# Second batch's reciprocals in step eight, gate rows ahead of the next rows' scaling, reciprocals' loads sent before the rows

## The reference, cut to what matters

```python
x = layernorm(x + attention(x, wq, wk, wv, wo))
# the feed-forward part, xf = x as 4096 rows
h = xf @ gw1.T + gb1
h = relu((h - mean(h)) * rsqrt(var(h) + 1e-5) * gamma + beta)      # 32 wide
gates = h @ gw2.T + gb2                                            # 8 wide
top_v, top_i = top_k(gates, 2); top_g = softmax(top_v)
onehot = (top_i[..., None] == arange(8)); counts = onehot.sum(axis=0)
w = einsum('nke,nk,ke->ne', onehot, top_g, counts <= capacity)
tmp = einsum('ni,eir->enr', xf, lora_A) * w.T[:, :, None]
out = xf @ weight.T + einsum('enr,ero->no', tmp, lora_B) / 16
x = layernorm(x + out)
```

## Time and profile before

| what | us |
|---|---|
| median of 3 runs | 3506.47 (3506.14 to 3508.07) |
| the profiled execution | 3506.97 |
| its span on the core | 3505.2 |
| mean granted clock of TensorE | 0.99 |

### The profile page before, as it was taken

The page is one execution under the profiler, slowest core; times in us unless marked ns, Lnnn a source line. Parts: engine busy times, 40 slices in busy tenths (PEclk is TensorE's granted clock), DMA queues, the critical chain, the costliest instruction groups (busy, mean ns, idle before and its releaser), DMA issues.

```text
span 3505.2 us, 61763 instructions
## 1 busy us (share of the span) xinstructions
PE 3426.8 (98%) x25202; PEld 2411.1 (69%) x25202; DVE 2013.6 (57%) x3618; ACT 1459.9 (42%) x1830; POOL 1743.8 (50%) x747
## 2 busy tenths in 40 slices
PE   8999998999999999999999999999998999999999
PEld 7888885566666666666665666666657888878887
DVE  3122116777777667677777767767655666642222
ACT  3111111555555555555555555555542332221111
POOL 0000002888988988898898898889550000000000
PEclk9999997999999999999999999999999999999999
DMA  6334325111121111112112111110037777654553
GB/s 214 114 123 120 113 90 127 26 51 48 32 54 50 35 42 50 42 34 51 48 32 54 50 31 47 50 38 11 26 106 217 234 234 234 211 201 173 173 173 130
DMA packets 248172, 340.60 MB, mean 97 GB/s; under 512 B 55520, under 2 KB 150240, under 8 KB 247904
## 3 DMA queue, kind: packets, MB, share of 16 engines
q1 hardware_dynamic: 247904, 336.87, 32.2%
HBM read 203.08 MB, written 133.17 MB: 96 GB/s over the span
## 4 chain that ended last, share of the span: by engine, by line
PE 78%; DVE 2%; ACT 2%; DMA 1%; issue 1%; POOL 0%; SPq 0%; ACTq 0%; POOLq 0%; DVEq 0%
PE p_o L682 19%; PE p_qm L647 17%; PE p_km L675 12%; PE p_acc L42 7%; PE p_acc L44 7%; PE p_acc L43 7%; PE p_km L668 3%; PE p_qm L651 2%; PE p_km L670 2%; ACT p_probs L759 2%; DVE p_part_max L795 1%; PE p_ag_ps L1096 1%; PE p_acc L1085 1%; DMA p_recip<-reciprocals 1%; PE p_ag_ps L1097 1%
## 5 line engine op out<-in xcount | busy, mean ns | idle before, releaser
L795 DVE TENSOR_REDUCE p_part_max<-p_qm 128x1 f32<-128x512 f32 (+3 forms) x2240 | 1407.0, 670 | 579.5 <-PE p_qm L647 328.8
L618 POOL TENSOR_TENSOR p_psums<-p_psums,p_probs 128x1024 f32<-128x1024 f32 x620 | 1479.3, 2386 | 93.3 <-ACT p_probs L755 2.8
L759 ACT ACTIVATE p_probs<-p_km 128x1024 f32<-128x1024 f32 x896 | 878.5, 1021 | 481.0 <-PE p_km L675 430.8
L647 PE MATMUL p_qm<-p_k_st,p_q_st 96*128 96x512 f32 (+3 forms) x2560 | 913.8, 421 | 12.4 <-DMA p_q_st<-q_hi 10.8
L647 PEld LDWEIGHTS p_qm<-p_k_st,p_q_st 96*128 96x128 f32 x2560 | 481.8, 195 | 254.2 <-issue 112.9
L675 PE MATMUL p_km<-p_q_st,p_k_st 97*128 97x512 f32 x1792 | 599.9, 417 | 13.5 <-ACT p_probs L759 8.7
L682 PE MATMUL p_o<-p_probs,p_v 128*32 128x256 f32 (+1 forms) x9216 | 565.5, 372 | 0.0
L682 PEld LDWEIGHTS p_o<-p_probs,p_v 128*32 128x32 f32 x9216 | 271.5, 110 | 216.7 <-issue 45.2
L675 PEld LDWEIGHTS p_km<-p_q_st,p_k_st 97*128 97x128 f32 x1792 | 312.1, 192 | 112.6 <-ACT p_probs L759 74.7
L614 POOL TENSOR_TENSOR p_psums<-p_probs 128x1024 f32<-128x1024 f32 x110 | 262.1, 2383 | 223.9 <-ACT p_probs L759 223.9
L33 POOL MEMSET p_ident<- 128x128 f32 x2 | 0.4, 204 | 551.0 <-POOLq L64 543.2
(11 more groups left out here) (153 smaller groups left out, 4004.0 us busy)
## 6 DMA issues: line engine op xcount, KB each, us to landing
p_q_st<-q_hi SPq DMA_DIRECT2D x128, 256.0 KB, 4.6
p_x_raw<-in_xT SPq DMA_DIRECT2D x64, 256.0 KB, 3.4
q_hi<-p_out_hi SPq DMA_DIRECT2D x64, 256.0 KB, 2.0
q_lo<-p_out_lo SPq DMA_DIRECT2D x64, 256.0 KB, 2.3
p_q_st<-q_lo SPq DMA_DIRECT2D x64, 256.0 KB, 4.3
attended_T<-p_o_raw SPq DMA_DIRECT2D x128, 128.0 KB
p_a_raw<-attended_T SPq DMA_DIRECT2D x32, 512.0 KB, 4.3
p_recip<-reciprocals SPq DMA_DIRECT2D x128, 128.0 KB, 6.6
```

The source lines that it names most:

```text
L618: pool.tensor_tensor(sums[:, :, :], sums[:, :, :], probs[(n * NS + s) % PB][:, :, :], ALU.add).then_inc(added, 1)
L647: last = pe.matmul(bank[:, x * keys:(x + 1) * keys], q_st[par][0:ROWS, c, h + x, sub * P:(sub + 1) * P], k_st[par][0:ROWS, j * CK:j * CK + ...
L759: act.activation(tile[:, :, :].rearrange("p h q -> p (h q)"), km[s % 2][:, :, :].rearrange("p a b -> p (a b)"), ACT.Exp, scale=SCALE).then ...
L795: dve.reduce_max(part_max[c][:, h:h + heads, sub, j], qm[bank_of(i)][:, 0:item_width(i)].rearrange("p (h k) -> p h k", h=heads), AX.X).the ...
```

## The change

Four things are changed.

1. The denominators of a batch are laid out as 128 x 512 instead of 64 x 1024 (`den0` on its first rows, `den1`), with four loads and four stores instead of two of each, in `Opening` and in `feed_forward`.
2. The second batch's reciprocal is taken out of the opening of VectorE's program. It is done in two halves of 128 x 256 at the ends of steps 6 and 7, stored by SP in step 8, and waited for in step 14, ahead of the loads of block 16.
3. VectorE does `hidden_out` and (from step 4 to the last block) `route` ahead of `divide_a` and `split_a`, with `route` between `hidden` and `hidden_out`; ScalarE does `hidden_root` ahead of `split_a`.
4. SP sends the four loads of reciprocals of block t+2 when block t+1 is scaled, and the load of the rows, behind them, when it is split.

```diff
--- before.py
+++ after.py
@@ -244,7 +244,7 @@
         self.a_raw, self.recip = sb("p3_a_raw", [P, KC, P]), sb("p3_recip", [P, KC, P])
         self.a_hi0 = sb("p3_a_hi0", [P, KC, P], F32R)
         with ExitStack() as until_split:
-            self.den0 = until_split.enter_context(nc.sbuf_tensor("p3_den0", [P, D], F32))
+            self.den0 = until_split.enter_context(nc.sbuf_tensor("p3_den0", [P, S // 4], F32))
         self.a_lo0 = sb("p3_a_lo0", [P, KC, P], F32R)
         with ExitStack() as until_last_chunks:
             tmp = lambda name, shape, dt=F32: until_last_chunks.enter_context(nc.sbuf_tensor(name, shape, dt))
@@ -272,16 +272,16 @@
         sp.dma_start(self.wo_raw[n][:, :], self.wo[n * P:(n + 1) * P, :]).then_inc(self.wo_in[n], 16)
 
     def load_denominators(self, sp):
-        for q in range(2):
-            sp.dma_start(self.den0[q * NH:(q + 1) * NH, :], self.den_d[:, q * D:(q + 1) * D]).then_inc(self.den_in[0], 16)
+        for q in range(4):
+            sp.dma_start(self.den0[q * NH:(q + 1) * NH, :], self.den_d[:, q * BANK:(q + 1) * BANK]).then_inc(self.den_in[0], 16)
 
     def send_reciprocals(self, sp):
         sp.wait_ge(self.rec_done[0], 1)
-        for q in range(2):
-            sp.dma_start(self.rec_d[:, q * D:(q + 1) * D], self.den0[q * NH:(q + 1) * NH, :]
+        for q in range(4):
+            sp.dma_start(self.rec_d[:, q * BANK:(q + 1) * BANK], self.den0[q * NH:(q + 1) * NH, :]
                          ).then_inc(self.rec_stored[0], 16)
         sp.dma_start(self.a_raw[:, :, :], self.aT_d[:, 0:P].rearrange("(k p) t -> p k t", p=P)).then_inc(self.a_in, 16)
-        sp.wait_ge(self.rec_stored[0], 32)
+        sp.wait_ge(self.rec_stored[0], 64)
         for h in range(REP):
             sp.dma_start(self.recip[h * HD:(h + 1) * HD, :, :],
                          self.rec_d[h:NH:REP, 0:P].unsqueeze(0).to_broadcast([HD, KC, P])).then_inc(self.a_in, 16)
@@ -301,8 +301,8 @@
             dve.tensor_tensor(self.wo_lo[:, n, :], self.wo_raw[n][:, :], self.wo_hi[:, n, :].bitcast(F32), ALU.subtract
                               ).then_inc(self.wo_lo_done, 1)
 
-        dve.wait_ge(self.den_in[0], 32)
-        dve.reciprocal(self.den0[0:2 * NH, :], self.den0[0:2 * NH, :]).then_inc(self.rec_done[0], 1)
+        dve.wait_ge(self.den_in[0], 64)
+        dve.reciprocal(self.den0[:, :], self.den0[:, :]).then_inc(self.rec_done[0], 1)
         for n in range(4):
             split_wo(n)
         dve.wait_ge(self.a_in, 16 * (1 + REP))
@@ -893,6 +893,8 @@
         weights = sb("p3_weights", [P, NT, E])
         second = sb("p3_second", [P, NT, E])
         LB = 4
+        with ExitStack() as first_pass:
+            den1 = first_pass.enter_context(nc.sbuf_tensor("p3_den1", [P, S // 4], F32))
         lowB = [sb(f"p3_lowB{i}", [P, ER]) for i in range(LB)]
         lw = [sb(f"p3_lw{i}", [P, ER]) for i in range(2)]
         lwT_hi = [sb(f"p3_lwT_hi{i}", [ER, P], F32R) for i in range(2)]
@@ -901,7 +903,7 @@
         YB, TB = 4, 3
         with ExitStack() as until_wm:
             tmp = lambda name, shape, dt=F32: until_wm.enter_context(nc.sbuf_tensor(name, shape, dt))
-            den1, ag_raw = tmp("p3_den1", [P, D])[:, :], tmp("p3_ag_raw", [P, KC, AG])[:, :, :]
+            ag_raw = tmp("p3_ag_raw", [P, KC, AG])[:, :, :]
         wm_hi, wm_lo = sb("p3_wm_hi", [P, KC, D], F32R), sb("p3_wm_lo", [P, KC, D], F32R)
         yB = [t[:, :] for t in opening.yB]
         lb_raw, lb_hi, lb_lo = opening.lb_raw[:, :], opening.lb_hi[:, :], opening.lb_lo[:, :]
@@ -956,6 +958,8 @@
             return 3 * n + 3
 
         assert wm_step(KC - 1) < NT - 2
+        REC_AT = 7
+        assert REC_AT + 1 < NT // B - 2
 
         def gpsimd(pool):
             over(pool)
@@ -968,6 +972,8 @@
             def load_a(t):
                 sp.dma_start(a_raw[:, :, :], aT_d[:, t * P:(t + 1) * P].rearrange("(k p) t -> p k t", p=P)
                              ).then_inc(a_in, 16)
+
+            def load_recip(t):
                 for h in range(REP):
                     sp.dma_start(recip[h * HD:(h + 1) * HD, :, :],
                                  rec_d[h:NH:REP, t * P:(t + 1) * P].unsqueeze(0).to_broadcast([HD, KC, P])
@@ -991,8 +997,8 @@
             load_x(0)
             load_x(1)
             sp.dma_start(ag_raw, ag.rearrange("(k p) r -> p k r", p=P)).then_inc(ag_in, 16)
-            for q in range(2):
-                sp.dma_start(den1[(2 + q) * NH:(3 + q) * NH, :], den_d[:, (2 + q) * D:(3 + q) * D]).then_inc(den_in, 16)
+            for q in range(4):
+                sp.dma_start(den1[q * NH:(q + 1) * NH, :], den_d[:, S + q * BANK:S + (q + 1) * BANK]).then_inc(den_in, 16)
             sp.dma_start(gw2T[:, :], gw2T_in).then_inc(small_in, 16)
             sp.dma_start(rows[:, :], rows_in.to_broadcast([P, ROWS])).then_inc(small_in, 16)
 
@@ -1010,14 +1016,17 @@
                     sp.wait_ge(y_done, u + 1)
                     sp.dma_start(y_t[u, :, :], y[u % 2][:, :]).then_inc(y_stored[u % 2], 16)
                 if t + 2 < NT:
+                    if t + 2 == NT // B:
+                        sp.wait_ge(rec_stored, 64)
+                    sp.wait_ge(a_done, t + 2)
+                    load_recip(t + 2)
                     sp.wait_ge(a_lo_done, t + 2)
                     load_a(t + 2)
-                if t == 1:
-                    sp.wait_ge(rec_done, 1)
-                    for q in range(2):
-                        sp.dma_start(rec_d[:, (2 + q) * D:(3 + q) * D], den1[(2 + q) * NH:(3 + q) * NH, :]
+                if t == REC_AT + 1:
+                    sp.wait_ge(rec_done, 2)
+                    for q in range(4):
+                        sp.dma_start(rec_d[:, S + q * BANK:S + (q + 1) * BANK], den1[q * NH:(q + 1) * NH, :]
                                      ).then_inc(rec_stored, 16)
-                    sp.wait_ge(rec_stored, 32)
                 for n in range(KC):
                     if t == wm_step(n) - 2:
                         if n > 0:
@@ -1246,10 +1255,10 @@
                     copy_hidden(t - 4)
                 if 1 <= t <= NT:
                     normalize(t - 1)
+                if 3 <= t < NT + 3:
+                    hidden_root(t - 3)
                 if t + 1 < NT:
                     split_a(t + 1)
-                if 3 <= t < NT + 3:
-                    hidden_root(t - 3)
                 for n in range(KC):
                     if t == wm_step(n):
                         split_wm(n)
@@ -1386,14 +1395,20 @@
                     scale_shift((t - 1) % 2, std_done, t, shift_done)
                 if 3 <= t < NT + 3:
                     hidden(t - 3)
+                if 4 <= t < NT:
+                    route(t - 4)
+                if 3 <= t < NT + 3:
+                    hidden_out(t - 3)
+                if NT <= t < NT + 4:
+                    route(t - 4)
                 if t + 1 < NT:
                     divide_a(t + 1)
-                if t + 1 < NT:
                     split_a(t + 1)
-                if 3 <= t < NT + 3:
-                    hidden_out(t - 3)
-                if 4 <= t < NT + 4:
-                    route(t - 4)
+                if t in (REC_AT - 1, REC_AT):
+                    cols = slice(0, BANK // 2) if t < REC_AT else slice(BANK // 2, BANK)
+                    if t < REC_AT:
+                        dve.wait_ge(den_in, 64)
+                    dve.reciprocal(den1[:, cols], den1[:, cols]).then_inc(rec_done, 1)
                 for n in range(KC):
                     if t == wm_step(n):
                         split_wm(n)
@@ -1430,8 +1445,6 @@
             dve.wait_ge(ag_hi_done, 1)
             dve.tensor_tensor(ag_w[:, :, AG:2 * AG], ag_raw, ag_w[:, :, 0:AG].bitcast(F32), ALU.subtract
                               ).then_inc(ag_lo_done, 1)
-            dve.wait_ge(den_in, 32)
-            dve.reciprocal(den1[2 * NH:4 * NH, :], den1[2 * NH:4 * NH, :]).then_inc(rec_done, 1)
             dve.wait_ge(small_in, 32)
             dve.wait_ge(experts_done, 1)
             for t in range(1, NT + 3):
```

## The result

The changed kernel takes 3493.10 us (median of 6 runs, 3490.32 to 3493.86), the kernel before 3506.43 beside it (6 runs, 3505.66 to 3508.07): a ratio of 0.9960, 95% interval 0.9948 to 0.9971, or 13.3 us less. The forecast was 12.4 less, 3494.1. The profiled execution took 3493.86 with a span of 3492.1, against 3505.2 before: 13.1 less.

What follows compares the result with a forecast made beforehand. TensorE, busy 98% of the span, was taken as the bound; removing two stalls of 4.65 and 7.8 us, other terms 0, took 12.4 from 3505.2 to a 3492.8 us span, 3494.1 as median; range 3491.5 to 3500.

Steps and rivals of the forecast that it cites:

- What was at stake: First pass of the feed-forward part: two TensorE stalls near 2632 and 2667 us, together 12.4 us, and nothing else.
- undisturbed step: TensorE's step from turn to turn, 14.46 us; without gate rows and a gate matmul pair, 12.03 us.
- The reciprocal leaves the opening: VectorE's opening: without the 6.55 us reciprocal, y is ready at 2626.8, 3.7 us before TensorE needs it.
- first stall: TensorE before the first turn of y: 2.9 us of wait plus the slow stretch behind it, 4.65 us.
- second stall: TensorE before the first turn of hidden rows: 5.7 us of wait plus 2.07 of slow clock, 7.8 us.
- Loads of blocks 3 and 4: Queue's sooner loads: blocks split by 2644.9 and 2658.1 at the slowest, cover 0.6 and 1.5 us, cost 0.
- The slowest of everything: Worst case for these loads: block 2 split at 2631.7, then 1.1 issue, 8.6 landing, 3.49 scaling and splitting.
- The moved reciprocals: VectorE, steps 6 and 7: two of 128x256, 1.6 us each by columns, 3.3 by elements; covered.
- The gate ahead of the scaling: VectorE's new order waits for TensorE's gate; gate to split 5.9 us, leaving 2.7 us of cover, cost 0.
- third rival: The gate makes scaled rows late in steps 4 to 30, beyond 2.7 us of cover: slower, e.g. 3521; chance 0.06.
- the first: Rival: TensorE waits for block 4's split rows instead of hidden rows; gain 5.3 to 9.3, 3497 to 3501; chance 0.10.

Runs made afterwards that it cites:

- layout only: Kernel before with only the second batch's denominators laid out as 128x512, one reciprocal still in the opening, its stores awaited in step 1: 3503.95 us, ratio 0.9990.
- order only: Kernel before with only the new order: gate rows ahead of scaling on VectorE, the root ahead of the split on ScalarE: 3505.65 us, ratio 0.9992.
- two more: Changed kernel with two idle 128x256 reciprocals on VectorE ahead of the scaling in steps 4 to 30: 3529.07 us, ratio 1.0058 to the kernel before.

## Why the prediction was right

**What was at stake**: right. Two stalls, each a wait and a slow stretch behind it, are all of the gain; 5.04 and 12.97 us at their two marks against 4.65 and 12.4. Most of the first difference is the undisturbed step: 2641.86 - 2630.08 = 11.78 us, where I had 12.03. I set the estimate by the Trainium skill (TensorE: Matmul & The Clock Gate, "HAM oscillation"), 13.7, aside for the 12.4 of the rows; the measured 13.1 of the span lies between them, and the spread of the runs doesn't tell which is nearer.

**The reciprocal leaves the opening**: right, and shown by half of it (layout only): 3.2 us less of VectorE ahead of y is enough for the first stall. In the changed kernel TensorE doesn't wait for y, with the turn at 2630.08.

**What ended the second stall**: here a step failed, though the number stood. "That removes what TensorE waited for at 2670" gave the second stall to VectorE's order. The order alone removes that wait and puts another of 3.8 us in its place; the queue's wait, moved alone, makes the hidden rows 3.9 us earlier with the order unchanged. I had read the 7.0 us of the earlier trace rows and written "that goes", at a cost of 0 and not as the gain. What I should have asked of the earlier trace rows: VectorE stood 5.76 us for block 4's loads, so when were those loads issued, and beside what. They were issued in time and landed late, in the crowd that the queue's wait had held back. The new order is insurance for hidden rows against late loads, and with early loads there is nothing to insure.

**Loads of blocks 3 and 4**: the end was right, a term was not. "The slowest of everything" took 8.6 us for a landing. Issued at 2629.31 and at 2642.69, the raw rows took these, from the transfers by issue of the changed kernel:

```profile
p_a_raw<-attended_T SPq DMA_DIRECT2D x1, 512.0 KB, 9.8
```

```profile
p_a_raw<-attended_T SPq DMA_DIRECT2D x1, 512.0 KB, 11.1
```

The bounds of 2644.9 and 2658.1 still held (2642.67 and 2657.44), because block 2 was split at 2629.28 and not at my 2631.7, so that everything started 2.4 us sooner. The two misses went against each other. Landings now end with the raw rows and no longer with the reciprocals (the bracket of VectorE's rows). The Trainium skill says in DMA: Bandwidth & Descriptors, "Queues, rings and completion order", that a transfer's semaphore write lands only after all earlier writes of its DMA engine, which agrees with this; but the raw rows are also issued last, and whether the rule or the plain load of the engines, at a DMA share of 0.75 to 0.79, sets the time, no run here separates.

**The moved reciprocals**: 1.75 us each, against 1.6 taken and 3.3 as the far bound. Their stores take the queue 5.42 us for four, above my 4.4; TensorE waited for nothing behind it. From the timelines of VectorE and of the queue, changed kernel:

```profile
2700.11 1.75 DVE L1411 RECIPROCAL p_den<-p_den 128x256 f32<-128x256 f32 x1
```

```profile
2729.83 5.42 SPq L1028 DMA_DIRECT2D reciprocals<-p_den  x4
```

**The gate ahead of the scaling**: right. VectorE now waits for TensorE's gate in 30 steps, 2.4 at the longest, and once more for 6.2 at the end of the pass. The third rival's mechanism is real: its break point lies a little nearer than I put it (2.3 to 2.5 against 2.7, as gate to split takes 6.05 us and not 5.9, and TensorE comes 0.1 sooner). The changed kernel stays 1.75 us or more away from it from step 4 on. In step 3, where loads decide, the cover is 1.5 us.

**Rivals**: the first showed itself in order only (a wait for split rows instead of hidden rows) and the third in two more; neither in the changed kernel. Not tried: both new orders together with the reciprocal left in the opening, and the halved reciprocal there together with the moved wait. So what the moving itself adds to these two isn't measured.

## What to carry to other kernels

A wait on the queue that issues transfers holds back all that is queued behind it and then lets it go at once, beside whatever is sent next. When an engine stands for a load, look at when that load was issued, what was issued just ahead of it, and what the queue stood for before that; and move such a wait to where its result is read. Reordering the engine that waits gains only what the load itself leaves, and a later release of a buffer comes back as a later load. A stall found in the trace is worth its wait plus the slow stretch behind it, read against an undisturbed step; who gets the credit for removing it takes a run with each cause removed alone, compared at the same mark and not by the spans of single executions.

## What the runs showed of the hardware

The reciprocal on VectorE went by columns, and 64 or 128 partitions made no difference: 64x1024 took 6.55 us, 128x512 3.35, 128x256 1.75. TensorE's granted clock went to 0.79 to 0.96 in stretches with or behind a wait of 2.7 us or more, and stayed at 1.00 where waits of about 1 us came 29 times (two more) and at the 1.7 us of the pass's end. The same 512 KB load landed in 8.6 us before and in 9.8 and 11.1 after, the latter beside a DMA share of 0.75 to 0.79. Four issues of reciprocals' loads took 5.37 us right behind five other transfers and 2.08 without them.
